# First attention: groups 0 and 1's row scores between projection pieces, rotation sums on GpSimd, weight split in the FFN

## The reference

```
x = x + 0.5 * L0_ffn(layernorm(x))
x = x + L0_attention(layernorm(x))      # 16 heads of 16, rotary, causal
x = x + 0.5 * L0_ffn(layernorm(x))
x = x + 0.5 * L1_ffn(layernorm(x))      # 6 blocks
x = x + L1_attention(layernorm(x))      # 16 query heads of 128, 4 key heads, causal
x = x + 0.5 * L1_ffn(layernorm(x))
```

```
q, k, v = h @ Wq.T, h @ Wk.T, h @ Wv.T              # h = layernorm(x); 2 batches x 16 heads
rope(y) = concat(y1 * cos - y2 * sin, y2 * cos + y1 * sin)
p = softmax(rope(q) @ rope(k).T / 4 + causal)
x = x + (p @ v) @ Wo.T
```

## Time and profile before

| | |
|---|---|
| runs | 2741.81, 2742.62, 2753.49 us; median 2742.62 |
| the profiled execution | 2735.0 us, its span 2733.2 us |
| TensorE busy (PE) | 2529.4 us, 93% |
| TensorE weight load (PEld) | 2111.5 us, 77% |
| VectorE busy (DVE) | 1847.8 us, 68% |
| ScalarE busy (ACT) | 1396.2 us, 51% |
| GpSimd busy (POOL) | 369.8 us, 14% |

### The profile page before, as it was taken

How to read it: one execution, slowest core, us unless ns; L and a number is a source line. 1 busy time by engine, 2 the same in 40 slices (tenths; PEclk the granted TensorE clock), 3 DMA queues, 4 the chain that set the end, 5 groups by cost and what they waited for, 6 DMA issues and landing times. The chain is left out here.

```text
span 2733.2 us, 49842 instructions
## 1 busy us (share of the span) xinstructions
PE 2529.4 (93%) x16744; PEld 2111.5 (77%) x16744; DVE 1847.8 (68%) x4018; ACT 1396.2 (51%) x2464; POOL 369.8 (14%) x279
## 2 busy tenths in 40 slices
PE   3975898869899999998999999999999999999999
PEld 3963445358788888887877877878877788888888
DVE  4566767456567777776766766767767677777773
ACT  3430555645455555554655655555555555555553
POOL 1000000010121222221110010001100222122220
PEclk9996989879999999999999999999999999999999
DMA  4026133000000000000000000000000000000000
GB/s 157 0 78 146 25 48 48 2 32 4 27 31 22 10 31 31 0 20 20 1 20 1 19 19 0 19 19 0 19 0 32 32 32 1 32 31 0 31 0 31
DMA packets 18930, 73.28 MB, mean 27 GB/s; under 512 B 3328, under 2 KB 8192, under 8 KB 15616
## 3 DMA queue, kind: packets, MB, share of 16 engines
q1 hardware_dynamic: 18816, 71.78, 9.2%
HBM read 61.02 MB, written 10.49 MB: 26 GB/s over the span
## 5 line engine op out<-in xcount | busy, mean ns | idle before, releaser
L349 PEld LDWEIGHTS ps<-w,hid 128*128 128x128 f32 x5376 | 698.9, 190 | 56.5 <-DVE rb L425 14.6
L349 PE MATMUL ps<-w,hid 128*128 128x256 f32 x5376 | 719.5, 284 | 2.5 <-DVE rb L425 1.5
L318 PE MATMUL ps<-xT,w 128*128 (+1 forms) x2688 | 703.9, 398 | 0.1
L502 DVE TENSOR_TENSOR hid<-gel,hid 128x512 fp32r<-128x512 f32 x448 | 403.4, 911 | 360.8 <-ACT hid L392 352.4
L386 ACT ACTIVATE gel<-ps,b 128x512 f32<-128x512 f32 x448 | 306.9, 686 | 557.3 <-issue 543.6
L318 PEld LDWEIGHTS ps<-xT,w 128*128 128x128 f32 x2688 | 479.6, 190 | 79.5 <-issue 0.3
L392 ACT ACTIVATE hid<-gel 128x512 fp32r<-128x512 f32 x448 | 272.9, 622 | 0.0
L864 PE MATMUL ps<-pT,v_sb 128*128 128x512 f32 (+3 forms) x1152 | 261.6, 358 | 1.9 <-DVE pT L982 1.9
L838 PE MATMUL ps<-k_sb,q_sb 128*128 128x512 f32 (+3 forms) x1152 | 252.7, 353 | 3.0 <-DVE q_sb L999 3.0
L971 DVE TENSOR_REDUCE negmax<-ps 128x1 f32<-128x128 f32 (+7 forms) x256 | 192.3, 752 | 76.8 <-PE ps L841 75.5
L1431 DVE TENSOR_REDUCE nmx<-ps 128x1 f32<-128x512 f32 (+3 forms) x384 | 196.2, 553 | 70.1 <-PE ps L1302 53.5
(11 more groups left out here) (118 smaller groups left out, 2884.1 us busy)
## 6 DMA issues: line engine op xcount, KB each, us to landing
wraw<-in_wffn SPq DMA_DIRECT2D x12, 2048.0 KB, 7.7
wraw<-in_w_a SPq DMA_DIRECT2D x8, 1280.0 KB, 5.4
qk_dram<-rope_hl SPq DMA_DIRECT2D x16, 512.0 KB, 3.0
xT<-qk_dram SPq DMA_DIRECT2D x60, 128.0 KB, 8.3
qk_own<-qk_dram SPq DMA_DIRECT2D x36, 128.0 KB, 6.4
xb<-in_wffn SPq DMA_DIRECT2D x2, 2048.0 KB, 13.0
x<-in_x SPq DMA_DIRECT2D x4, 512.0 KB, 5.5
rot<-in_rot SPq DMA_DIRECT2D x1, 2048.0 KB, 18.7
```

The costliest lines, as they stand in the source:

```text
L318: last = nc.tensor.matmul(ps[:, HPS + j % 4, :], w[par][:, wp, 0, k * HIDDEN + j * PART:k * HIDDEN + (j + 1) * PART], xT[:, xp, k, bass.ds ...
L349: last = nc.tensor.matmul(y_ps[:, t, :], hid[:, hp, j % 4, t * PART:(t + 1) * PART], w[par][:, wp, 1, j * DIM:(j + 1) * DIM], start=j == 0 ...
L502: nc.vector.tensor_tensor(hid[:, 1, j % 4, :], gel[:, j % 4, :], hid[:, 0, j % 4, :].bitcast(f32), ALU.subtract).then_inc(low_done, 1)
```

## The change

- **Weights.** The four copies of `act_split_a0` and the four subtractions of `dve_split_a0` move into steps j = 4 to 7 of the first FFN's first chunk. For that `w_qkv`, `w_o` and the other buffers of attention 0 have new places in SBUF; `qk_own` becomes `q_own` and `k_own`, and the products read these.
- **Tail and pieces are words of the plan.** `S` is the last chunk's second product and take, `P` a piece, `L` a part of the last chunk's norm, `G` its transposes, affine and low part. The pieces are listed as the first batch's half 0, its half 1, then the second batch. `S` stands first, norm parts stand behind pieces 0 to 3, `G` behind piece 3. Pieces 0 to 7 wait only for the first two chunks' `xT`.
- **Values** come two tiles at a time behind pieces 4 to 11, both into bank 6 (`AV0_PS`).
- **Row scores** of groups 0 and 1 stand three pairs behind each piece from piece 6 on, the last two of the 32 behind those.
- **Rotation.** The sum and the low part go from VectorE to GpSimd (`pool_rope_a0`), with the memsets of `k_own` and `v_f` behind sum 1 and low 0, `nmx` behind low 1, and the first half of `xT` behind piece 9's.
- **Loads.** Group 0's heads are issued behind store 4, group 1's behind store 9, group 2's behind store 15 and the 2 MB load.

The diff, cut (buffer renames, the unchanged bodies of moved functions and imports of names are left out; line numbers of the changed program are some 5 to 50 higher):

```diff
...
         def pe_tail(pe, p):
-            if p.k == 2:
+            if p.k in (0, 2):
                 return
...
+                if p.k == 0 and prev is None and 4 <= j < 8:
+                    act_split_a0(act, j - 4)
...
+                if p.k == 0 and prev is None and 5 <= j < 8:
+                    dve_split_a0(dve, j - 5)
+                    if j == 7:
+                        dve_split_a0(dve, 3)
...
-        PIECES = [(qk, half) for qk in range(2) for half in range(KD)]
-        N_PIECES = BATCH * CHUNKS // 2 * len(PIECES)
+        PIECES = [(chunk, qk, half) for chunks, halves in (((0, 1), (0,)), ((0, 1), (1,)), ((2, 3), (0, 1)))
+                  for chunk in chunks for half in halves for qk in range(2)]
+        N_PIECES = len(PIECES)
+        V_FROM, U_FROM, U_EACH = 4, 6, 3
...
+        def pool_rope_a0(pool):
+            def low_part(n):
+                pool.wait_ge(rope_high, n + 1)
+                nc.gpsimd.tensor_tensor(rope_hl[:, 1, n % 2, :], rope[:, 2, n % 2, :],
+                                        rope_hl[:, 0, n % 2, :].bitcast(f32), ALU.subtract).then_inc(rope_low, 1)
+
+            def ones(buffer):
+                nc.gpsimd.memset(buffer[1].bitcast(f32), 1.0).then_inc(k_ones, 1)
+
+            pool.wait_ge(mm2_done, HT * CHUNKS)
+            for n in range(N_PIECES):
+                pool.wait_ge(rope_taken, n + 1)
+                if n >= 2:
+                    pool.wait_ge(rope_low, n - 1)
+                nc.gpsimd.tensor_tensor(rope[:, 2, n % 2, :], rope[:, 0, n % 2, :], rope[:, 1, n % 2, :],
+                                        ALU.add).then_inc(rope_sum, 1)
                 if n:
                     low_part(n - 1)
+                if n == 1:
+                    ones(QK[0])
+                    nc.gpsimd.memset(v_f[:], 1.0).then_inc(v_ones, 1)
+                if n == 2:
+                    nc.gpsimd.memset(nmx[:], 0.0).then_inc(v_ones, 1)
+                if n == 9:
+                    pool.wait_ge(proj_ready, 8)
+                    pool.wait_ge(v_ready, QT // 2)
+                    ones(QK[1])
             low_part(N_PIECES - 1)
...
-                if n == N_PIECES // 2:
+                if n == 4:
                     for stored in rope_stored:
-                        sp.wait_ge(stored, 16 * N_PIECES // 4)
+                        sp.wait_ge(stored, 32)
                     sp.wait_ge(k_ones, 1)
                     load_heads(0)
-
-            rope_pieces(sp, piece)
+                if n == 9:
+                    sp.wait_ge(k_ones, 2)
+                    load_heads(1)
             sp.wait_ge(a_low, 4)
             load(1, 0, xb_raw)
             sp.wait_ge(k_ones, 3)
-            for g in (1, 2):
-                load_heads(g)
+            load_heads(2)
...
-            for j in range(T_GROUP + AHEAD):
+            todo.append(("S",))
+            norm = {0: (0,), 1: (1,), 2: (2, 3), 3: (4, 5)}
+            for n in range(N_PIECES):
+                todo.append(("P", n))
+                todo += [("L", k) for k in norm.get(n, ())]
+                if n == V_FROM - 1:
+                    todo.append(("G",))
+                if n >= U_FROM:
+                    for j in range((n - U_FROM) * U_EACH, min((n - U_FROM + 1) * U_EACH, T_GROUP + AHEAD)):
+                        rows_of(j)
+            for j in range((N_PIECES - U_FROM) * U_EACH, T_GROUP + AHEAD):
                 rows_of(j)
...
```

More of the change, by code:

```diff
@@ L1133, in dve_project_a0, with rope_piece @@
-        def dve_project_a0(dve):
-            def low_part(n):
-                dve.wait_ge(rope_high, n + 1)
-                nc.vector.tensor_tensor(rope_hl[:, 1, n % 2, :], rope[:, 2, n % 2, :],
-                                        rope_hl[:, 0, n % 2, :].bitcast(f32), ALU.subtract).then_inc(rope_low, 1)
-            def piece(n, token, seq, qk, half, slot):
-                dve.wait_ge(proj_ready, n + 1)
-                for term in range(2):
-                    nc.vector.tensor_tensor(rope[:, term, slot, :], ps[:, 2 * slot + term, :],
-                                            rot[:, 2 * qk + term, seq:seq + CHUNK], ALU.mult)\
-                        .then_inc(rope_taken if term else rope_term, 1)
+        def rope_piece(n):
+            chunk, qk, half = PIECES[n]
+            return chunk * CHUNK, chunk * CHUNK % SEQ, qk, half, n % 2
@@ new lines, in value_pair, with act_split_a0, dve_split_a0 @@
+        def value_pair(n):
+            return n - V_FROM if 0 <= n - V_FROM < TILES // 2 else None
+        def act_split_a0(act, piece):
+            act.wait_ge(a_loaded, 16)
+            tile, to, of = a0_split(piece)
+            nc.scalar.activation(tile[:, 0, to], xb_flat[:, of], ACT.Copy).then_inc(a_high, 1)
+        def dve_split_a0(dve, piece):
+            tile, to, of = a0_split(piece)
+            dve.wait_ge(a_high, piece + 1)
+            nc.vector.tensor_tensor(tile[:, 1, to], xb_flat[:, of], tile[:, 0, to].bitcast(f32), ALU.subtract)\
+                .then_inc(a_low, 1)
@@ L1388, in output @@
                 last.then_inc(ring_ready, 1)
-            run_a0(dict(U=rows, T=tiles, A=weighted, N=turn_maxima, C=turn_context, E=turn_back, O=output))
+            run_a0(dict(S=second_tail, P=piece, G=lambda: pe_transpose_chunk(pe, tail(phase(0))[1]),
+                        U=rows, T=tiles, A=weighted, N=turn_maxima, C=turn_context, E=turn_back, O=output))
         def act_attend_a0(act):
@@ L1474, in output, with piece @@
                     .then_inc(ring_free, 1)
-            dve.wait_ge(v_ones, 2)
-            run_a0(dict(U=rows, J=join_maxima, N=low_maxima, C=normalise, E=low_context, O=output))
+            p, at = phase(0), tail(phase(0))
+            norm = dve_norm(dve, at[1], at[2], False, 0, at[1] - p.s0 + p.norms0)
+            def piece(n):
+                token, seq, qk, half, slot = rope_piece(n)
+                dve.wait_ge(proj_ready, n + 1)
+                if n >= 2:
+                    dve.wait_ge(rope_sum, n - 1)
+                for term in range(2):
+                    nc.vector.tensor_tensor(rope[:, term, slot, :], ps[:, 2 * slot + term, :],
+                                            rot[:, 2 * qk + term, seq:seq + CHUNK], ALU.mult)\
+                        .then_inc(rope_taken if term else rope_term, 1)
+            dve.wait_ge(att_tab, 16)
+            run_a0(dict(S=lambda: dve_take(dve, p, at), P=piece, L=lambda k: norm[k](),
+                        G=lambda: dve_low_input(dve, at[1], at[2]), U=rows, J=join_maxima, N=low_maxima, C=normalise, E=low_context, O=output))
         steps_raw = rb[:, 1:TPC, :].rearrange("p t e -> p (t e)")[:, 0:STEPS]
@@ L1615, in _ @@
                 walk(p, act, lambda at, prev: act_step(act, p, at, prev))
[L1616 to L1618 removed]
+                if k == 1:
                     act_affine(act, tail(p)[1], CHUNKS - 1, 0)
```

193 lines of the change are left out of this document (89 added, 104 removed).

## The result

Median 2785.4 us of seven runs (2773.4 to 2807.7) against 2741.8 of the kernel before (2731.6 to 2760.0): ratio 1.0158, 95% interval 1.0122 to 1.0194, so 43 us slower. The forecast was 2756.1 with a range to 2778, which the time lies outside. Slower by over 13.7 had a chance of 0.43, second to no measurable change.

What follows compares the result with a forecast made beforehand. TensorE, half busy at a clock of 0.52 for 48.5 us of row scores, was to be filled; tail, loads, loop and maxima put attention's first tile at 289 against 275.5, +13.5, giving a median of 2756.1 us, range 2731 to 2778.

Steps and rivals of the forecast that it cites:

- last sentence of the prediction: Wrong if the first tile starts before 278, or if the stretch behind it no longer takes as long as before.
- Part 1: Splitting w_a0 in the first FFN: 0 us, covered by ScalarE's idle time; without that cover 3 us of copies.
- Part 2: Tail up to store 4: GpSimd holds eight small VectorE instructions about 1 us each; norm applied at 166.5, store at 181.
- Part 3: Heads' loads behind store 4: they take 14 us, a new wait with TensorE idle from about 182 until 195.5.
- Part 4: Interleaved loop of pieces, values and row scores: 61 us at full clock plus 5 throttled; piece 15 ends at 261.5.
- clock's rival: TensorE's clock stays at 1.2 GHz in the interleaved loop: +19 us, first tile at 308, 2775 us; chance 0.15.
- Part 5: Behind piece 15: group 0's maxima queue behind store 15, weight load and heads; some 18 us of new wait for TensorE.
- Sum: First tile of attention at 289 against 275.5, +13.5 us; profiled execution 2748.5, median 2756.1.
- rows hidden: Row scores cost TensorE only their issue, 1.5 us a group, not 3.0; first tile at 265.5, 2732 us; chance 0.20.
- Maxima not held up: Small maxima transfers land while the bulk loads are under way; first tile at 282.3, 2749 us; chance 0.15.

Runs made afterwards that it cites:

- rows from 9: The changed kernel with row scores from piece 9 on, four pairs behind a piece; median 2788.2 us, ratio 1.0156 to the kernel before.
- memsets later: The changed kernel with the memsets of k_own, v_f and nmx behind low part 2 and the norm's end; median 2782.2 us.
- early maxima: The changed kernel with group 0's eight maxima transfers issued behind store 13, ahead of store 15 and the weight load; median 2747.4 us.

## Why the prediction was wrong

- **"Behind that tile both programs have the same steps in the same order. So the forecast is: when does that first tile start?"** This is the step that failed. The steps are the same; where ScalarE's instructions lie is not, and that cost 19.4 us in attention 1; one instruction put back took 13.3 us off the median. Nine instructions fewer on ScalarE were to be had from the built program, and a loop of 325 in it; no term, bound or rival had them. The last sentence of the prediction named this as what would prove it wrong.
- **Part 1**: right, piece 0 starts at 145.25 (145.1 forecast), so the split costs nothing that shows.
- **Part 2**: right in kind, too small. Transposes at 170.8 (166.5 forecast). Six small instructions were held, not eight; five were 1.1 to 1.3 (1 forecast), but one was 6.84: I had priced a hold by one GpSimd instruction, and it spanned three. The products (1.29 a pair) and the loop's reductions (1.29) weren't held, a GpSimd sum of 512 columns took 1.26 to 1.30 (1.27 taken).
- **Part 3**: right, 14.46 of idle time (14 forecast). The first pair came at 201.8 instead of 195.5: 4.3 of that is the late tail, 1.0 lies between it and store 4, and the loads took 15.5 from their first issue to the pair (14.5 forecast).
- **Part 4**: right within 2: 68 us from the first pair to the end of piece 15 at a mean clock of 0.91 (66 forecast, 5 of it for the clock). The rows from 9 and the memsets later show how near it was to the clock's rival.
- **Part 5**: right, 20.8 of wait (18 and more forecast), nearly all of it taken away by issuing eight small transfers earlier.
- **Sum**: first tile at 296.4, forecast 289, +20.8 for +13.5. By that alone the median would have been near 2763, inside the range.
- **Rivals**: rows hidden: against, 0.82 to 0.87 of idle time stay at a hand-over of 512 columns, and 1.6 at one in each of the last periods. Maxima not held up: against. The clock of the loop: not in the changed kernel, yes in two of its relatives.

## What to carry to other kernels

When work is moved, its transfers move in a queue too: both new waits of TensorE (14.5 and 20.8 us) came from there, and the second went with the place of eight small issues. When a change touches one stage, compare the others all the same, loop by loop, with the packets of the instruction queues beside them (45 against 69 on the page): the place of a long loop's code cost 14 to 19 us here, or 4 in another bad place, and hung on one instruction. And ask of a hit whether it has one cause: the early maxima gained 38 us, of which some 18 (by the traces' loads) came from the one instruction that the edit added by the way.

## What was not expected of the hardware

- One instruction of satisfied waits on ScalarE was worth 13.3 us in the median and 14.4 to 18.5 in the loop of attention 1.
- A VectorE instruction of 4 columns was held for 6.84 us over three GpSimd instructions in a row.
- Half clock behind 22 us of idle time lasted 24 us, with TensorE busy for 23 of them, and yet a hold of 23.1 us cost 22.8 in the median (interval 15 to 40); the throttled stretches further on in attention 0 move about from one execution to the next (302 to 333 us for the same steps). What sets them was not settled.
